# Summing a scan's states: a third accumulating DMA in place of TensorE, and a PSUM bank moved to attention

## The reference

```python
# xc, z, dt: (B, L, 512); Bm, Cm: (B, L, 16)
dA  = exp(dt[..., None] * A)
dBx = dt[..., None] * Bm[:, :, None, :] * xc[..., None]
h = dA_t * h + dBx_t            # for each token t, channel d, state n
y = einsum('bdn,bn->bd', h, C_t)
y = y + xc * D                  # the skip term
out = y * silu(z) @ W_out
```

## Time and profile before

| | us |
|---|---|
| median of 3 runs | 1382.21 |
| lowest, highest | 1377.51, 1398.91 |
| the profiled execution | 1379.84 |
| its span, first to last instruction | 1377.9 |
| TensorE busy (matmul), weight loads | 1160.8, 921.4 |
| VectorE busy | 1056.9 |
| ScalarE busy | 794.5 |
| POOL busy | 290.7 |

### The profile page before, as it was taken

The page is one execution under the profiler, slowest core; times in us unless marked ns, Lnnn a source line. Parts: engine busy times, 40 slices in busy tenths (PEclk is TensorE's granted clock), DMA queues, the critical chain, the costliest instruction groups (busy, mean ns, idle before and its releaser), DMA issues.

```text
span 1377.9 us, 16592 instructions
## 1 busy us (share of the span) xinstructions
PE 1160.8 (84%) x5760; PEld 921.4 (67%) x5760; DVE 1056.9 (77%) x1719; ACT 794.5 (58%) x1989; POOL 290.7 (21%) x341
## 2 busy tenths in 40 slices
PE   4697677888899799989998899988998989989852
PEld 2454456666678577866786678867786768868741
DVE  3998899899869797899879897998699763343216
ACT  3433545467658665677567756776477545536521
POOL 0000201222421333232313231324122420010001
PEclk9877999989999899999999999999999999999976
DMA  4612010234424424234414442533343320000301
GB/s 183 242 46 71 7 63 8 77 77 92 101 54 92 89 47 115 58 81 99 110 31 100 86 96 55 110 76 60 92 104 77 50 51 20 1 0 8 121 0 61
DMA packets 55285, 100.27 MB, mean 73 GB/s; under 512 B 5417, under 2 KB 28810, under 8 KB 54562
## 3 DMA queue, kind: packets, MB, share of 16 engines
q0 software_dynamic: 27648, 37.76, 16.8%
q1 hardware_dynamic: 27554, 61.46, 13.8%
HBM read 55.42 MB, written 6.04 MB: 45 GB/s over the span
## 4 chain that ended last, share of the span: by engine, by line
PE 40%; DVE 31%; DMA 9%; ACT 9%; issue 7%; POOL 4%; DVEq 0%; SPq 0%; ACTq 0%; POOLq 0%
PE bank L288 15%; DVE scans L520 10%; DMA scans<-scans 9%; PE bank L1105 4%; DVE scans L516 4%; DVE scans L523 4%; PE bank L1150 3%; PE bank L1123 3%; PE bank L475 2%; DVE nmax L1259 2%; DVE conv L399 2%; PE bank L671 2%; PE bank L883 2%; ACT scans L498 2%; PE bank L889 1%
## 5 line engine op out<-in xcount | busy, mean ns | idle before, releaser
L520 DVE TENSOR_TENSOR_SCAN scans<-scans 128x1024 f32<-128x1024 f32 x128 | 292.3, 2284 | 16.4 <-ACT scans L498 11.9
L498 ACT ACTIVATE scans<-dt,a_neg 128x255 f32<-128x255 f32 x512 | 221.4, 500 | 0.0
L475 PE MATMUL bank<-scans,ident 128*128 128x256 f32 x448 | 138.7, 432 | 49.9 <-DMA scans<-scans 27.0
L1193 ACT ACTIVATE ya<-bank,nmax 128x256 f32<-128x256 f32 x256 | 107.1, 472 | 86.1 <-DVE nmax L1259 86.0
L523 DVE TENSOR_TENSOR scans<-scans,BC 128x1024 f32<-128x1024 f32 x128 | 155.7, 1217 | 1.2
L1259 DVE TENSOR_REDUCE nmax<-bank 128x2 f32<-128x512 f32 x128 | 87.3, 683 | 90.2 <-PE bank L1105 89.1
L516 DVE TENSOR_TENSOR scans<-conv,BC 128x1024 f32<-128x1024 f32 x128 | 155.7, 1216 | 0.1
L552 POOL DMA_DIRECT2D scans<-scans x96 | 84.1, 876 | 289.1 <-DMA scans<-scans 287.8
L475 PEld LDWEIGHTS bank<-scans,ident 128*128 128x128 f32 x448 | 87.8, 210 | 85.5 <-DMA scans<-scans 38.9
L1123 PE MATMUL bank<-v,ya 128*128 128x65 f32 x1024 | 135.5, 278 | 4.4 <-ACT yo L1184 4.4
L1123 PEld LDWEIGHTS bank<-v,ya 128*128 128x128 f32 x1024 | 132.6, 201 | 8.3 <-issue 5.9
(11 more groups left out here) (255 smaller groups left out, 2229.6 us busy)
## 6 DMA issues: line engine op xcount, KB each, us to landing
BC<-xpj_scratch SPq DMA_DIRECT2D x32, 1024.0 KB, 6.1
scans<-scans POOLq DMA_DIRECT2D x96, 256.0 KB, 3.4
scans<-scans POOLq DMA_DIRECT2D x96, 128.0 KB, 2.7
xin<-in_x SPq DMA_DIRECT2D x8, 256.0 KB, 4.3
conv<-in_x SPq DMA_DIRECT2D x8, 256.0 KB, 2.9
out<-scans SPq DMA_DIRECT2D x8, 256.0 KB, 2.7
kept_x<-x SPq DMA_DIRECT2D x7, 256.0 KB, 2.0
kept_w<-wa SPq DMA_DIRECT2D x7, 256.0 KB, 2.0
```

The source lines that it names most:

```text
L475: last = pe.matmul(sums_of(c), ident[:, :], step_of(b, u)[:, i, :], start=False, stop=(h == UH - 1 and i == SUMMED[b] - 1), skip_group_che ...
L498: ins = act.activation(step[:, j, 1:S], dt[b % 2][:, c, 1:S], ACT.Exp, scale=a_neg[:, c, n:n + 1])
L520: dve.tensor_tensor_scan(flat(H[:, :, :]), flat(H[:, :, :]), flat(dBx), 0.0, ALU.mult, ALU.add).then_inc(s["a_scan"], 1)
L1193: act.activation(pe_[:, h % 2, t, :], YB[h % 2][:, t * S:(t + 1) * S], ACT.Exp, bias=nmax[:, h % 4, t:t + 1]).then_inc(s["t_p"], 1)
```

## The change

- The two DMAs of a unit are followed by a third: it adds the one remaining state, 128 KB, onto `xc` of the unit's chunk, in SBUF (`store_pool`). All three are used from batch 1 on; batch 0 keeps the four matmuls a unit. Each of the three kinds has one semaphore (`a_two`, `a_one`, `a_sum`), and POOL waits for the landing of the DMA of the same kind of the unit before. The three kinds are streams of their own on POOL: S, A (`fold_pool`) and B (`store_pool`).
- `xc` has two buffers now. When dtx is made from it, ScalarE multiplies it by D in place (four instructions a batch, `a_skip`), so that it holds the skip term; the diagonal matrices and their matmuls are gone. VectorE's gating reads `xc` in place of PSUM, in two pieces behind the last unit; in batch 0 it first adds the sums from PSUM (two instructions).
- exp of the unit three later waits for `a_sum`, the landing of the third DMA, in place of the matmul.
- `SA` is now banks 1 and 7 (7 for batch 0 alone); the out-projection has bank 1. Attention has banks 4 to 7: its transposes always go to `y3`, bank 7. Scores of head h wait for the exp of head h - 2 (`t_p`) and no more for the copy; the transposes of a head wait for the copy of the head before.
- Small things: `b_ho` is loaded at the end into a part of `xnT`; the small layer norm tiles are parts of one; a semaphore `b_tT` is merged into `b_vT`.
- The whole `ORDER` is written anew.

```diff
-SUMMED = (4, 4, 1, 1, 1, 1, 1, 1)
...
     "pool": (
-        "FFSFWWWFSSWSSSWSSSSSSSSSSSSSSSSSSSSSSSWSWYSWSSSFWSSSSSSSSWSSSWSSSSSSSSSSSSSFSSSSSWWYSWSSSSWSSSSSSSSSWSSSWSSSSS"
-        "SSSSSSSSSSSWWYSWSSFSWSSSSSSSSWSSSWSSSSSSSSSSSSSSSSSSSWSWYWSFSSWSSSSSSSSSWSSSWSSSSSSSSSSSSSSSWSWYSWSSSWSSSSSSSS"
+        "FFSSWASBABWSFASBASBABSASBASBASBASBASBAWBSASBABSABSASBFABSSASBWASBAWBSASBASBABSABSASBASBYASBASBASBWABSWWASABSAB"
...
-        xc = sb("xc", [P, EC, S])
+        xc = [sb(f"xc{i}", [P, EC, S]) for i in range(2)]
...
-        skips = sb("skips", [P, EC, P])
...
-        SA = bank[1:3]
+        so = bank[1]
+        SA = [so, bank[7]]
...
-                act.wait_ge(*of("a_skip_ps", b - 1))
+            if b >= 2:
+                act.wait_ge(*of("a_gated", b - 2))
...
+            act.wait_ge(*of("a_dtx", b))
+            for c in range(EC):
+                act.activation(xc[b % 2][:, c, :], xc[b % 2][:, c, :], ACT.Copy, scale=d_skip[:, c:c + 1]).then_inc(s["a_skip"], 1)
...
+        def by_dma(name, b, u):
+            return s[name], 16 * (NU * (b - 1) + u + 1)
+        def of_sum_of(b, u):
+            return by_dma("a_sum", b, u) if b else (s["a_y_ps"], u + 1)
...
         def scan_pe(pe, b):
-            pe.wait_ge(*of("a_xc", b))
-            if b:
+            if b == 0:
+                for u, (h, c) in enumerate(UNITS):
+                    pe.wait_ge(*of("a_hC", b, u + 1))
+                    for i in range(HN):
+                        last = pe.matmul(sums_of(c), ident[:, :], step_of(b, u)[:, i, :], start=(h == 0 and c % 2 == 0 and i == 0),
+                                         stop=(h == UH - 1 and i == HN - 1), skip_group_check=True)
+                    last.then_inc(s["a_y_ps"], 1)
+                    yield
+            else:
                 pe.wait_ge(*of("a_res", b - 1))
-            else:
-                pe.wait_ge(s["prep_skips"], EC)
-            for c in range(EC):
-                last = pe.matmul(sums_of(c), skips[:, c, :], xc[:, c, :], start=(c % 2 == 0), stop=False, skip_group_check=True)
-            last.then_inc(s["a_skip_ps"], 1)
-            yield
-            for u, (h, c) in enumerate(UNITS):
-                if SUMMED[b] == HN:
-                    pe.wait_ge(*of("a_hC", b, u + 1))
-                else:
-                    pe.wait_ge(*of_sum(b, u, ADDS[SUMMED[b]]))
-                for i in range(SUMMED[b]):
-                    last = pe.matmul(sums_of(c), ident[:, :], step_of(b, u)[:, i, :], start=False, stop=(h == UH - 1 and i == SUMMED[b] - 1),
-                                     skip_group_check=True)
-                last.then_inc(s["a_y_ps"], 1)
-                yield
             pe.wait_ge(*of("a_gated", b))
             if b == 0:
                 pe.wait_ge(s["loads_first"], N_FIRST)
             for t in range(T):
-                last = mm(pe, SA[0][:, t * D:(t + 1) * D], [(zg[b % 2][:, c, t * P:(t + 1) * P], w_out[:, c, :]) for c in range(EC)])
+                last = mm(pe, so[:, t * D:(t + 1) * D], [(zg[b % 2][:, c, t * P:(t + 1) * P], w_out[:, c, :]) for c in range(EC)])
...
-                if NU * b + u >= 3:
-                    act.wait_ge(s["a_y_ps"], NU * b + u - 2)
+                g = NU * b + u
+                if g >= 3:
+                    act.wait_ge(*of_sum_of((g - 3) // NU, (g - 3) % NU))
...
-                if u == NU - 2:
-                    dve.wait_ge(*of("a_y_ps", b, NU - 2))
-                    dve.wait_ge(*of("a_silu_z", b))
-                    z = flat(zg[b % 2][:, 0:2, :])
-                    dve.tensor_tensor(z, SA[0][:, :], z, ALU.mult).then_inc(s["a_gated"], 1)
-                    yield
-            dve.wait_ge(*of("a_y_ps", b))
-            z = flat(zg[b % 2][:, 2:4, :])
-            dve.tensor_tensor(z, SA[1][:, :], z, ALU.mult).then_inc(s["a_gated"], 1)
-            yield
+            for i in range(2):
+                z, y = [flat(x[:, 2 * i:2 * i + 2, :]) for x in (zg[b % 2], xc[b % 2])]
+                dve.wait_ge(*of("a_silu_z", b))
+                dve.wait_ge(*of("a_skip", b))
+                dve.wait_ge(*of_sum_of(b, NU - 4 + 2 * i))
+                dve.wait_ge(*of_sum_of(b, NU - 3 + 2 * i))
+                if b == 0:
+                    own.link(dve.tensor_tensor(y, SA[i][:, :], y, ALU.add))
+                dve.tensor_tensor(z, y, z, ALU.mult).then_inc(s["a_gated"], 1)
+                yield
...
         def scan_pool(pool, own, b):
-            def folded(u):
+            for u in range(NU if b else 0):
                 pool.wait_ge(*of("a_hC", b, u + 1))
+                if (b, u) > (1, 0):
+                    pool.wait_ge(*by_dma("a_two", b, u - 1))
                 H = step_of(b, u)
-                pool.dma_start(flat(H[:, 0:2, :]), flat(H[:, 2:4, :]), accum_op=ALU.add).then_inc(SUM_OF[(NU * b + u) % 3], 16)
-            def folded_again(u):
-                pool.wait_ge(*of_sum(b, u, 1))
-                H = step_of(b, u)
-                pool.dma_start(H[:, 0, :], H[:, 1, :], accum_op=ALU.add).then_inc(SUM_OF[(NU * b + u) % 3], 16)
-            for u in range(NU if SUMMED[b] < HN else 0):
-                folded(u)
-                yield
-                if SUMMED[b] == 1:
-                    folded_again(u)
-                    yield
+                pool.dma_start(flat(H[:, 0:2, :]), flat(H[:, 2:4, :]), accum_op=ALU.add).then_inc(s["a_two"], 16)
+                yield
             pool.wait_ge(*of("a1_var", b))
             rstd(pool, own, "a1").then_inc(s["a1_rstd"], 1)
             yield
 
-        w0, w1 = bank[3:5]
+        def fold_pool(pool, b):
+            for u in range(NU if b else 0):
+                pool.wait_ge(*by_dma("a_two", b, u))
+                if (b, u) > (1, 0):
+                    pool.wait_ge(*by_dma("a_one", b, u - 1))
+                H = step_of(b, u)
+                pool.dma_start(H[:, 0, :], H[:, 1, :], accum_op=ALU.add).then_inc(s["a_one"], 16)
+                yield
+        def store_pool(pool, b):
+            for u in range(NU if b else 0):
+                h, c = UNITS[u]
+                pool.wait_ge(*by_dma("a_one", b, u))
+                pool.wait_ge(*of("a_skip", b, c + 1))
+                if (b, u) > (1, 0):
+                    pool.wait_ge(*by_dma("a_sum", b, u - 1))
+                pool.dma_start(xc[b % 2][:, c, :], step_of(b, u)[:, 0, :], accum_op=ALU.add).then_inc(s["a_sum"], 16)
+                yield
+        w0, w1 = bank[2:4]
...
-        y0, y1, y2 = bank[5:8]
+        y0, y1, y2, y3 = bank[4:8]
...
-                    pe.wait_ge(*of("t_pT", b, h - 1))
+                    pe.wait_ge(*of("t_p", b, 2 * h - 2))
...
             def turned(h):
                 pe.wait_ge(*of("t_p", b, 2 * h + 2))
+                if h:
+                    pe.wait_ge(*of("t_pT", b, h))
                 for k in range(2):
                     for t in range(T):
-                        last = pe.transpose(YB[h % 2][:, k * S + t * P:k * S + (t + 1) * P], pe_[:, h % 2, t, k * P:(k + 1) * P], ident[:, :])
+                        last = pe.transpose(y3[:, k * S + t * P:k * S + (t + 1) * P], pe_[:, h % 2, t, k * P:(k + 1) * P], ident[:, :])
                 last.then_inc(s["t_pT_ps"], 1)
...
-                    act.activation(pT[:, h % 2, :, :].rearrange("p a b -> p (a b)"), YB[h % 2][:, :], ACT.Copy).then_inc(s["t_pT"], 1)
+                    act.activation(pT[:, h % 2, :, :].rearrange("p a b -> p (a b)"), y3[:, :], ACT.Copy).then_inc(s["t_pT"], 1)
...
```

118 lines of the change are left out of this document (55 added, 63 removed).

## The result

| | before | after |
|---|---|---|
| median of 4 runs, us | 1381.72 | 1403.82 |
| lowest, highest | 1377.51, 1398.91 | 1398.78, 1407.6 |
| ratio, 95% interval | | 1.0172 [1.0134, 1.0211] |
| profiled execution, span | 1379.84, 1377.9 | 1407.6, 1405.8 |

The change makes the kernel 1.7% slower. The forecast was 1328 us with a range up to 1372: the time is outside it and on the other side.

A forecast was written before the change was run, and what follows sets the result against it. TensorE was taken to lead the middle regime, with VectorE idle behind it. From the profiled 1379.8 us, -61 + 15 + 0 - 8 = -54 gave 1326, as a median 1328 us; range 1275 to 1372.

The forecast's parts named there:

- main term: From 258 to 1138 us: with TensorE relieved, VectorE leads at 92% density, 819 us in place of 880, so -61 us.
- What VectorE waits for says who leads: Middle regime: VectorE's largest wait, 32.9 us, is for attention's scores, so TensorE leads and VectorE stands 127 us idle behind it.
- The sums' 62.5 us of busy rows: TensorE, 258 to 1138 us: removing the sums' 96 matmuls (192 records) was counted as 62.5 us less work.
- The 27.0 us of waits: TensorE, 258 to 1138 us: its queue's standstill for the DMAs ahead of the sums, 27.0 us, was counted as saved.
- The 15 us for the scores' bank: TensorE in attention: scores no longer wait for the copy of head h - 2; saving taken as 15 us, ends 0 and 28.
- Batches 0 and 1: Start of the kernel: TensorE loses 33.3 us of sums in batch 1, but VectorE leads; 0 us, ends -5 and +12.
- The ring: Step buffers: the third DMA lengthens a lap by 2.2 us, 0.9 us short in dense pieces; +15 us, ends 0 and +45.
- if it waits for ScalarE's first column behind the third DMA: Sign that the forecast is wrong: VectorE waiting for ScalarE's first column behind the third DMA; no size given.
- The rival "slower": Middle batches: 24 collisions with BC loads at 3.7 us, 89 us, no longer absorbed by the ring; 1431 us; chance 0.06.
- POOL: POOL's queue: a third issue of 0.9 us a unit, 86 us added to 256 of 880, called covered.
- The clock: TensorE, middle: a granted clock falling from 0.97 to 0.94 makes 764 us 788, under 819; no time by itself.
- The tail: After 1138 us: fewer columns in TensorE's queue and less waiting for the copy; -8 us, ends -20 and 0.

The follow-up runs named there:

- e4: Kernel before, own order, without the sum matmuls on TensorE in batches 2 to 7, buffer free with the second DMA's landing: ratio 0.9859.
- e11: Kernel before, own order, with neither sum matmuls nor DMAs from batch 1 on, buffers free after the product with C: ratio 0.9862.
- e3: Kernel after without any of a unit's three DMAs, buffer free once the product with C is made: ratio 0.9976.
- e2: Kernel after without the third DMA, buffer free with the second landing: ratio 0.9976.
- e13: Kernel after with the third DMA reading a constant, so the buffer is free with the second landing; gating still waits for the third: ratio 1.0039.
- e10: Kernel before without the sum matmuls and with the product with C for two of four states, batches 2 to 7: ratio 0.9745.
- e14: Kernel before without sum matmuls in batches 2 to 7, plus a third DMA behind the next unit's first; buffer free with its landing: ratio 1.1417.
- e12: Kernel before, complete, with 16 of its 96 single sum matmuls one place later in TensorE's queue: ratio 0.9984.
- e8: Kernel after with a second bank for attention's transposes, 56 of the 64 odd heads using the out-projection's bank: ratio 1.0186.
- e5: Kernel before, own order, without batch 1's 64 sum matmuls on TensorE: ratio 0.9998.
- e6: Kernel after with 64 dummy matmuls on TensorE in batch 1, four a unit, nobody waiting for them: ratio 1.0186.
- e7: Kernel after with dummy matmuls on TensorE, four a unit in batch 1 and one a unit in batches 2 to 7: ratio 1.0205.
- e9: Kernel before with VectorE's product with C made for two of the four states in batches 2 to 7: ratio 0.9862.

## Why the prediction was wrong

The parts of the change, by ratios to the kernel before, each with some 5 to 7 us of uncertainty. They are differences of one row of ratios, so their sum is the measured change by construction:

| part | forecast | measured | from |
|---|---|---|---|
| main term (measured: sums off TensorE) | -61 | -19 | e4, e11 |
| new order, bank, skip term, gating: batch 1 | 0 | +21 | e11, e3 |
| the same: middle | in the main term | +7 | e11, e3 |
| the same: tail | -8 | -12 | e11, e3 |
| first two DMAs in it | 0 | 0 | e3, e2 |
| third DMA in POOL's queue | in the ring's term | +9 | e2, e13 |
| third DMA on the lap | +15 in all | +18 | e13, after |
| sum | -54 | +24 | |

**The step that failed is the main term**: "At the density that it reached where TensorE didn't lead, 92% [...], that is 753.3 / 0.92 = 819 us. This is above TensorE's 764, so VectorE takes the lead". TensorE did get lighter, but VectorE didn't pack denser: 87% in e4, 83% after. The maximum's wait for scores, which was to be less than 32.9 us, is 38.4 in the middle of the kernel after. The 92% came from a stretch with no attention heads beside the scans: the first maximum (L1259) of the kernel before starts at 266.2 us. With the sums gone VectorE's idle time in the middle fell only from 127 to 113 us, so most of it wasn't TensorE's load in another place. What fits the timelines is the latency of chains that pass VectorE, ScalarE, TensorE and POOL in turn, each through an in-order queue. The evidence against a leader is e10, where both reliefs add up. The reading "What VectorE waits for says who leads" took a wait for scores, 32.9 of the 127 idle us, as TensorE being late by its load. In the timelines of the kernel after and of e14 shown here TensorE is late because ScalarE stands at a lap's first column. For the kernel before that isn't shown.

**The terms within it.** The sums' 62.5 us of busy rows were 32.8 when they went (e4). The weight loads' 32.7 us came out nearer; their own fall was 25.5. A part of the missing 30 us may be the clock: at 0.95 in place of 0.97 the other 730 us of rows would be 2% longer, 15 us, by my estimate from these rows. In the kernel after 74 us of rows went and busy time in the middle fell by 23.6. The Trainium skill (Perfetto Trace Analysis, Identifying the Most-Contended Engine) calls matmul busy percent no good measure for TensorE, and this case agrees as far as the relief was smaller than the rows. That VectorE would be the bound by that measure isn't borne out: each relief gave 19 us. The 27.0 us of waits: 8 of them removed were no gain by themselves (e12), and ScalarE's wait for the same buffers grew by 15. The 15 us for the scores' bank: no price could be put on it alone; e8 shows that a second bank for the transposes adds nothing.

**Batches 0 and 1** were given 0, from -5 to +12, because VectorE led there. They cost 21. The trace of e3 shows two parts: 8.5 us of VectorE's work of other streams moved into batch 1 (115.87 in place of 107.32 us busy in e11), and some 13 more us of its idle time. The prediction counted 5 us of other streams' work more, without saying clearly of which engine, and put it at nothing. Where VectorE sets the pace, its own pieces are the ones to count. Of the idle time some 10 us lie behind the last unit, where the second gating instruction stands behind attention's first maxima (e3's timeline above). That too could have been read from the new queue.

**The ring.** The size was about right (18 by the lap, with 0 to 45 as ends), and that is in part luck, since the path was another: VectorE's scans wait 18.7 us for ScalarE in the middle, under the forecast's 20 to 45, and the price came through ScalarE's own wait. The prediction did name that wait, "if it waits for ScalarE's first column behind the third DMA", as a sign of being wrong, but on VectorE and without a price. The price of a long lap goes by what is queued behind L488. The rival "slower" had the sign, but its price (24 collisions with BC loads at 3.7 us, 89 us) isn't what happened: by the count above some 11 of ScalarE's 71.4 us stand beside such a load. The order's cost in batch 1 stood in no rival.

**POOL** was called covered. 9 us is small but not nothing. The issue times did as the row said: 977 ns mean for the first DMA, 894 for the second, against 941 and 876, and the longest first issue 1257 ns against 1241, so the stall of the DMA issue of which the Trainium skill warns (SBUF — State Buffer, SBUF: two separate sides) doesn't show in this trace either.

**The clock** fell further than expected (0.91 in place of 0.94). It cost nothing in batch 1 (e5, e6). In the middle no run changes it by itself: e7 bounds only the clock and the lighter load together.

**The tail** was 222 us against 228 to 240 forecast. It is the one window that gained by the new order: its TensorE and VectorE work is less (172.8 in place of 184.3 us, 85.0 in place of 87.1), and more of it stands in earlier windows.

Left open: whether moving the second gating instruction back would give its 10 us back in batch 1, which pieces cost the rest, whether e4's 19 us come from TensorE's load or from the buffer's earlier release, and what the bank is worth by itself in the old order. No version here beats both kernels with the reference's whole computation done; e4, e9, e10 and e11 leave work out.
